# Decoder layer on one core: four products of the attention block move to the fill banks, with another order on four engines

## The reference

```python
def attn(x, Wq, Wk, Wv, proj_w, proj_b):          # 16 heads of 64; q, k, v are taken as (heads, batch, t, hs) by reshape
    wei = jnp.einsum('hbqd,hbkd->hbqk', q, k) * hs ** (-0.5)
    wei = softmax(where(causal, wei, -inf))
    out = einsum('hbqk,hbkd->hbqd', wei, v).reshape(b, t, h * hs)
    return out @ proj_w.T + proj_b
def xattn(q, k, v, mask, w_q, w_k, w_v, w_o):     # 16 heads of 16, 77 keys
    Q, K, V = proj(q, w_q), proj(k, w_k), proj(v, w_v)
    attn = softmax(where(mask == 0, NEG, Q @ K.T / 4))
    return (attn @ V) @ w_o.T
x = layernorm(x + attn(x, ...))                   # x1 in the kernel
x = layernorm(x + xattn(x, ctx, ctx, mask, ...))  # x2
x = layernorm(x + moe(x, ...))
```

## Time and profile before

| | us |
|---|---|
| runs | 1498.46, 1499.05, 1501.37 |
| median | 1499.05 |
| profiled execution | 1499.4 |
| its span in the trace | 1497.7 |
| first y1 (L1045), last y1, last logits copied (L1086) | 76.3, 976.7, 999.3 |
| busy in the span: PE, DVE, ACT, POOL | 1299.9, 1083.6, 923.6, 724.8 |

### The profile page before, as it was taken

The page is one execution under the profiler, slowest core; times in us unless marked ns, Lnnn a source line. Parts: engine busy times, 40 slices in busy tenths (PEclk is TensorE's granted clock), DMA queues, the critical chain, the costliest instruction groups (busy, mean ns, idle before and its releaser), DMA issues. The chain is left out here.

```text
span 1497.7 us, 47409 instructions
## 1 busy us (share of the span) xinstructions
PE 1299.9 (87%) x16821; PEld 1078.5 (72%) x16821; DVE 1083.6 (72%) x3112; ACT 923.6 (62%) x2287; POOL 724.8 (48%) x974
## 2 busy tenths in 40 slices
PE   4789999999999999999999998755899999999930
PEld 2577788788778878878887887632688888888820
DVE  4778888888888888888888888658455555555537
ACT  3656787787777777777777766514344444444426
POOL 3245556655664664565566544420244444334326
PEclk9999999999999999999999999985999999999975
DMA  9654757667668667767677665029332354332335
GB/s 239 108 92 99 168 146 165 158 175 155 147 168 175 141 152 191 152 146 200 137 161 163 157 114 106 18 97 419 97 79 73 78 165 92 76 77 71 74 143 204
DMA packets 292448, 208.95 MB, mean 140 GB/s; under 512 B 218782, under 2 KB 249630, under 8 KB 289792
## 3 DMA queue, kind: packets, MB, share of 16 engines
q1 hardware_dynamic: 278784, 180.87, 50.7%
q0 software_dynamic: 7136, 18.76, 4.3%
q10 hardware_dynamic: 6304, 6.29, 1.4%
HBM read 93.79 MB, written 65.93 MB: 107 GB/s over the span
## 5 line engine op out<-in xcount | busy, mean ns | idle before, releaser
L1753 PE MATMUL ps_e<-xt,wres 128*128 128x128 f16 x3408 | 343.2, 220 | 6.1 <-DMA xt<-xg 5.1
L1753 PEld LDWEIGHTS ps_e<-xt,wres 128*128 x3408 | 285.4, 98 | 78.1 <-issue 6.9
L1817 ACT ACTIVATE act_g<-ps_e,b 128x128 f32<-128x128 f32 x568 | 162.2, 368 | 208.3 <-PE ps_e L1753 206.2
L1760 PE MATMUL ps_e<-wres,g_hi 128*128 x568 | 214.5, 379 | 0.8 <-DVE g_lo L1840 0.8
L753 ACT ACTIVATE probs<-st_k,nmax 128x128 f32<-128x128 f32 (+1 forms) x512 | 199.9, 448 | 2.2 <-DVE nmax L983 1.9
L1720 POOL DMA_INDIRECT z_scr<-e_y,dst_i x71 | 85.1, 1198 | 210.2 <-DVE e_y L1831 207.0
L983 DVE CUSTOM_DVE_ANT_0 st_k<-ps,causal 128x128 f32<-128x128 f32 (+1 forms) x512 | 160.6, 351 | 28.6 <-PE ps L452 28.6
L760 ACT ACTIVATE pt_hi<-ps 128x384 f16<-128x384 f32 x256 | 125.0, 488 | 55.4 <-PE ps L460 29.9
L1762 PE MATMUL ps_e<-wres,g_lo 128*128 x568 | 154.8, 273 | 0.0
L460 PE MATMUL ps<-ident,probs 128*128 128x128 f32 x768 | 131.2, 280 | 24.5 <-ACT probs L753 19.5
L988 DVE TENSOR_TENSOR pt_lo<-ps,pt_hi 128x384 f16<-128x384 f32 x256 | 141.3, 552 | 6.1 <-ACT pt_hi L760 2.7
(11 more groups left out here) (285 smaller groups left out, 4042.2 us busy)
## 6 DMA issues: line engine op xcount, KB each, us to landing
k_pair<-k_pair SPq DMA_DIRECT2D x96, 256.0 KB, 6.5
st_p<-in_moe_w SPq DMA_DIRECT2D x24, 768.0 KB, 6.4
w_scr<-st_p SPq DMA_DIRECT2D x24, 768.0 KB, 4.2
wres<-w_scr SPq DMA_DIRECT2D x18, 1024.0 KB, 22.8
v_scr<-v_tok SPq DMA_DIRECT2D x32, 512.0 KB, 5.3
v_pos<-v_scr SPq DMA_DIRECT2D x64, 256.0 KB, 5.8
q_st<-st_q SPq DMA_DIRECT2D x64, 128.0 KB, 2.8
z_scr<-zero SPq DMA_DIRECT2D x32, 256.0 KB, 6.6
```

Of the source, the lines that this page charges most:

```text
L1753: last = mm(out, w(c * FF + f * P, b, P), xt[:, t % X_BUFS, a, c], start=(m == 0), stop=(m == 5))
L1760: mm(out[:, 0:2 * D], g_hi[:, t % G_BUFS, f], w(KC * FF + f * D, 0, 2 * D), start=(f == 0), stop=False, skip_group_check=True)
L1817: nc.scalar.activation(act_g[:, k % 2, f], ps[:, 3 + 2 * (k % 2) + f // 4, (f % 4) * P:(f % 4 + 1) * P], ACT.Gelu, bias=bias[:, f:f + 1], ...
```

## The change

Four results leave the banks c5 and c6 for the fill banks: the turned output uses `ps_a[1]` and `ps_a[0]` (its first half is now copied by VectorE, its second by ScalarE), the projection, the turned x1 and the query product `ps_a[0]`. The second attention's scores and probabilities, the context products and the value rows keep c5 and c6. The fills use the banks by a table, and their waits follow it. `o_norm` gets two buffers, so that VectorE waits for the split of the pair before the last. Each `step(s)` on PE, ACT, DVE and POOL is written in another order and cut at another place.

```diff
+FILL_BANK = (1, 0, 1, 0, 1, 1)
-    o_norm = sb("o_norm", [P, 4, HS], F32)
+    o_norm = sb("o_norm", [P, 2, 4, HS], F32)
...
-            if since(t, 1) or j >= 2:
+            if j == 0 and since(t, 1):
+                pe.wait_ge(s_fill_lo, NF * t)
+            if j == 1 and since(t, 3):
+                pe.wait_ge(s_q2_lo, t - 2)
+            if j in (2, 3):
                 pe.wait_ge(s_fill_lo, NF * t + j - 1)
-            bank = ps_a[j % 2]
+            if j == 4:
+                pe.wait_ge(s_fill_lo, NF * t + 3)
+                if since(t, 2):
+                    pe.wait_ge(s_ot_d, t - 1)
+            if j == 5:
+                pe.wait_ge(s_fill_lo, NF * t + 5)
+            bank = ps_a[FILL_BANK[j]]
...
             if g == 0:
                 pe.wait_ge(s_o_lo, 4 * (t + 1))
-                if since(t, 1):
-                    pe.wait_ge(s_t2_lo, 4 * t)
-                for half_, bank in enumerate((c5, c6)):
+                pe.wait_ge(s_fill_lo, NF * (t + 2) + 4 if has(t + 2) else NF * TILES)
+                for half_, bank in enumerate((ps_a[1], ps_a[0])):
...
-                        last = mm(c5[:, 0:D], o_t[:, :, h], wp[:, k, h], start=(h == 0 and k == 0), stop=(h == H - 1 and k == 1))
+                        last = mm(ps_a[0][:, 0:D], o_t[:, :, h], wp[:, k, h], start=(h == 0 and k == 0), stop=(h == H - 1 and k == 1))
...
-            if since(t, 1) or g > 1:
-                dve.wait_ge(s_o_lo, pair)
-            nc.vector.tensor_tensor(o_norm[:], o[:, :, 1:1 + HS],
+            if since(t, 1) or g > 3:
+                dve.wait_ge(s_o_lo, pair - 1)
+            nc.vector.tensor_tensor(o_norm[:, pair % 2], o[:, :, 1:1 + HS],
```

More of the change, by code:

```diff
@@ L221, in run @@
     def run(step, once={}):
-        for s in range(-4, TILES + 4):
+        for s in range(-6, TILES + 6):
             if s in once:
@@ L620, in step @@
         def step(s):
-            if has(s):
+            if has(s + 1):
+                fill(s + 1, 1)
+            if has(s - 1):
+                scores(s - 1, 7)
+                turn_probs(s - 1, 5)
+            if has(s - 3):
+                stage_d(s - 3, 4)
+            if has(s - 2):
+                stage_c(s - 2, 5)
+            if has(s - 1):
+                pv(s - 1, 4)
+                turn_probs(s - 1, 6)
+                pv(s - 1, 5)
+            if has(s - 2):
+                if s - 1 != TILES:
+                    stage_c(s - 2, 6)
+            if has(s - 1):
+                turn_probs(s - 1, 7)
+            if has(s + 1):
+                fill(s + 1, 2)
+            if has(s):
+                scores(s, 0)
+            if has(s - 2):
+                if s - 1 != TILES:
+                    pv2(s - 2, 0)
+            if has(s - 1):
+                pv(s - 1, 6)
+            if has(s):
+                scores(s, 1)
+            if has(s - 1):
+                pv(s - 1, 7)
+            if has(s + 1):
+                fill(s + 1, 3)
+            if has(s):
+                scores(s, 2)
                 turn_probs(s, 0)
-                scores(s, 2)
-            if has(s - 1):
-                stage_c(s - 1, 0)
             if has(s - 2):
-                pv2(s - 2, 1)
+                stage_c(s - 2, 7)
+                if s - 1 == TILES:
+                    pv2(s - 2, 0)
             if has(s):
@@ L912, in step @@
                 hi(s + 2, 2)
+            if s == 0:
+                late_split(7)
+            if has(s + 1):
+                exps(s + 1, 0)
             if has(s - 1):
@@ L916, in step @@
             if has(s + 1):
[L917 removed]
+                exps(s + 1, 1)
+            if has(s):
+                o_high(s, 7)
+            if has(s + 2):
+                hi(s + 2, 3)
             if has(s - 1):
                 stage_c(s - 1, 7)
+            if has(s + 1):
+                pt(s + 1, 0)
             if has(s):
[L921 to L923 removed]
+                stage_c(s, 0)
         def causal_mask():
@@ L1380, in step @@
                 split_o(s, 7)
+            if s == 0:
+                value_constants()
+            if has(s):
+                bias_x(s)
+            if s == -1:
+                constants()
             if has(s) and even(s):
                 spread_k2(s, 0)
+                spread_k2(s, 1)
+            if has(s):
+                inverse_deviation(s, 0, s_mv1, s_rstd1)
+            if has(s + 3):
+                split_x(s + 3)
+            if has(s - 1):
+                inverse_deviation(s - 1, 1, s_mv2, s_rstd2)
+            if 0 <= s - 3 < PIECES:
+                piece_low(s - 3, 0)
+            if has(s):
+                own_values(s, 0)
+            if has(s + 1):
+                split_o(s + 1, 1)
+            if has(s):
+                shift(s, 0)
+            if has(s + 1) and even(s + 1):
+                split_context(half(s + 1))
+            if has(s - 1):
+                split_x2(s - 1)
+            if 0 <= s - 3 < PIECES:
+                piece_low(s - 3, 1)
+            if has(s + 1):
+                split_o(s + 1, 3)
         pool.sem_inc(s_w_out, 16)
         pool.sem_inc(s_w_lo, 1)
-        run(step, {-1: constants, 1: value_constants})
+        run(step)
 def weight_rows(io):
```

361 lines of the change are left out of this document (150 added, 211 removed).

## The result

The changed kernel takes 1515.03 us (median of 4 runs, 1513.8 to 1516.22), the kernel before on the same chip 1498.76 (4 runs, 1498.43 to 1501.37). The ratio is 1.0105, with a 95% interval of 1.0087 to 1.0122: slower, where no change was forecast. The time is the one that rival 2 named, 1515 us. The profiled execution took 1516.22 us with a span of 1514.5.

The account below looks back on a forecast made before the run. It took a ring to bound the kernel: y1, VectorE's list to the turned output, the projection, y1 again. Tiles gave -1.9 us, start -1.5, end +1.7: forecast 1497.5 us, no change that can be told, range 1490 to 1505.

Parts of the forecast that it names:

- rival 2: GpSimd's list joins the ring: a late second shift delays ScalarE, then k's last low half; slower, 1515 us, chance 0.22.
- DMAs: SyncE's chain of value, key and query transfers lands 1.9 us before the scores need it: no cost.
- three signs of being wrong: x2 stays at 0.41 us, ScalarE waits over 1 us a tile for the second shift, or group 0's scores await a DMA.
- The walk: One odd tile followed through all new lists from y1, each instruction starting when engine and input are ready; intervals 28.6 and 29.7.
- o2_lo's new wait: VectorE waits for ScalarE's o2_hi, the turned second output's high half: 0.95 us a tile, bounds 0.6 and 1.2.
- TensorE's stand for o2_norm: Behind pv2, TensorE issues nothing until VectorE's o2_norm is there, ahead of the projection: 0.9 to 1.0 us a tile.
- x1: VectorE's first norm product, held by GpSimd's x_up, takes 0.87 us and not 0.40.
- Rival 4: x1 is held through three GpSimd instructions, to 4.07 and not 2.84, about 0.8 a tile: slower, 1523 us, chance 0.02.
- The ledger: VectorE's tile as busy time plus waits, 29.05 us before; the change's parts were priced in it, giving 29.14 with a piece.
- o_norm's 0.77: VectorE's wait for GpSimd's o_st before o_norm, 0.77 us a tile, goes to 0 with two buffers.
- the held x2's 0.76: VectorE's x2 beside GpSimd's low part of a piece takes 1.17 us, not 0.41: 0.76 more in 24 tiles.
- rival 1: The two norms on VectorE aren't held by GpSimd, which takes off 18.2 us and about 2: faster, 1477 us, chance 0.24.

Follow-up runs that it names:

- e1: Changed kernel, but SyncE issues the load of a context at the end of its step before: 1499.96 us, ratio 1.0002.
- e12: Kernel of e1 with GpSimd's second shift of the maxima behind its next split of the output instead of ahead of it: 1507.59 us, ratio 1.0046.
- e5: Kernel of e1 with the first part of the piece's low half on GpSimd behind the product that spreads the second values: 1495.87 us, ratio 0.998.
- e9: Kernel of e5, but in tiles without the second values' product the piece's first part stands behind the split of the output: 1493.98 us, ratio 0.9964.
- e4: Kernel before the change with the two buffers of o_norm alone: 1497.14 us, ratio 0.9983.
- e6: Kernel of e1 with the second attention's turned output behind the projection, ScalarE's half behind the expert weights: 1498.51 us, ratio 0.9991.
- e3: Changed kernel with GpSimd's context split behind the projection's bias, turned second output behind the projection, ScalarE's half ahead of the expert weights: 1580.06 us.
- e8: Changed kernel with the load of a context issued later, behind the three query transfers: 1574.27 us.

## Why the prediction failed

*The step that failed* is the one headed "DMAs". It walked SyncE's chain of values, keys and queries, found 1.9 us of slack and wrote "No cost". The load of the context stands in the same list, behind the doubling, and its consumer had moved from 16.5 to 11.6 us after y1. What the runs put in its place: seven stands of 1.4 to 2.9 us and one stretch at half clock, 16.8 us, all of which e1 takes away. A check of that one transfer would have found it: issue 5.7 to 9.9 us after y1 in the tiles of before, landing 2.5 later in the median, against a split at 11.6: late wherever it is issued after 9.1.

The 1.9 us were mis-sized as well. In the changed kernel's tiles from 200 to 900 us the last query transfer lands 12.6 to 17.7 us after y1, and the scores come at 17.15: slack of 3 us in some tiles and none in three. Of the prediction's three signs of being wrong, one was there in three tiles (the scores of group 0 waited for a DMA) and one in the seven long tiles alone (ScalarE waited 2.0 us in their mean for the second shift, 0.6 over all).

*Rival 2* had the place, the chain and the rate. The walk's 0.3 us of slack behind the second shift are less than 0.1 in tiles with a context (at 18.2 us) and at least 0.45 in the others (e12). Its condition, a shift late by its own list in all 24 tiles, was not met; the transfer made it late in seven. That both come to 1515 is chance.

*The walk* of the lists was right: 28.6 and 29.7 forecast, 28.68 and 29.77 measured. So were x2 at 1.2 us, o2_lo's new wait (22.0 us in 23 tiles, 0.96), TensorE's stand for o2_norm (0.9) and y1's wait for the projection (44.2 in 23, 1.92). At the start the first y1 came 2.0 sooner (1.5 forecast; e1, e5 and e9, alike up to there, have it at 73.2, 71.9 and 73.8 us, so part of it may be scatter) and the first interval is 27.66 against 31.56 (2.2 forecast, 3.9 measured); the end is 2.2 longer (1.7).

*x1* was mis-sized: 0.87 us forecast beside the split of x, 0.44 measured. Rival 4, built on it, falls.

*The ledger* was wrong as a reason. It added VectorE's waits and priced each at its length. o_norm's 0.77 was worth nothing in the intervals (e4), the held x2's 0.76 was worth 0.27 in tiles with a context (e9), though 0.23 of 0.29 in the others (e5), and o2_lo's 0.95 was worth 0.05 to 0.09 (e6). Only the walk through all the lists, which carries every engine, gave the intervals. The sum agreed with the walk because its last terms, blocking, projection and "other", were taken from the walk. For that reason rival 1's price was too high too: e9 took 13 us off x2 in the 24 tiles and gave 6.

## What to carry to other kernels

When an order moves a consumer forward, look up every transfer that it reads and where its issue stands in the DMA queue; a transfer that lands in time in most tiles is late in some, and a queue's head shows it only there. Where several engines close a ring with nearly equal length, what is added behind the end of the slack costs its full length (e12), and what is removed gives only as much as the next path is shorter: 0.23 of 0.29 us in e5, 0.27 of 0.79 in e9, nothing in e4. Price a removal by walking all lists again. And a waiting instruction at the head of an in-order list costs by what is queued behind it: the same move on TensorE cost 73 us in e3 and gave about 1.5 in e6.

## What the hardware showed that was not expected

VectorE's x1 ran in 0.44 us beside GpSimd's multiplication by a constant (x_up, one input, 0.86 us) in all 21 cases from 200 to 900 us in which that instruction overlapped it whole, and GpSimd had begun 0.1 us earlier. Alone it takes 0.40. Beside GpSimd's products of two inputs the same form was held to 0.91 (own values) and 1.20 us (the piece's low part). The Trainium skill ("SBUF — State Buffer", Who interferes with whom) has VectorE, when its instruction uses the ports that it shares with GpSimd, and GpSimd block each other for the whole instruction of the one that starts first; that agrees with the products of two inputs and not with the one of one input.

TensorE's clock fell to 1.2 GHz for some seven us in one of the changed kernel's seven long tiles, where it had stood for 0.68 and 1.20 us within three us, and not in the one where it had stood for 1.30 and 1.20. In e8 it fell in ten tiles. In e12 it fell once, for 3.4 us, in a tile whose stands (0.53, 0.85 and 0.81 us) were those of the other tiles, and that interval took 1.7 us more. In both tiles with a mean of 0.90 that are shown above, 2.6 us came on top of the stand. What decides between the tiles isn't shown.
